# Expert tail: the token table from one-hot products, rows gathered inside the expert stage, one round of experts, answers gathered in two passes

## The reference

```
ln1 = _ln(hidden_states, ln1_weight, ln1_bias)            # attention over the 16 rows that share a column
hidden_after_attn = hidden_states + attn_out @ proj_weight.T
x = _ln(hidden_after_attn, ln2_weight, ln2_bias).reshape(-1, H)     # 4096 tokens, H = 128
probs = softmax(x @ router_weight)                        # 8 experts
top_p, top_i = top_k(probs, 2); top_p = top_p / sum(top_p)
order = argsort(top_i.reshape(-1)); within = position of a pick among its expert's picks
cap = ceil(N * 2 / 8 * 1.25)                              # 1280 slots of each expert, 10240 in all
keep = within < cap; slot = where(keep, expert * cap + within, 8 * cap)
padded_tokens = zeros(8 * cap + 1, H).at[slot].set(x[order // 2])
act = gelu(einsum('ech,ehf->ecf', exp_in, moe_w1))        # F = 512, exact gelu
exp_out = einsum('ecf,efh->ech', act, moe_w2)
moe = zeros(N, H).at[padded_ids].add(exp_out * padded_probs)
out = _layernorm(x_before + hidden_after_attn + moe)
```

## Time and profile before

| | |
|---|---|
| median of 3 runs | 2252.81 us (2251.59 to 2257.84) |
| the profiled execution | 2237.28 us |
| its span, first to last instruction | 2235.5 us |
| granted TensorE clock, mean | 0.88 of full speed |
| busy TensorE, VectorE, ScalarE, GpSimd | 1786.7, 1367.8, 1232.4, 1044.3 us |

### The profile page before, as it was taken

One profiled execution on the slowest core, in us unless ns is written; L12 is line 12 of the kernel. 1 busy time (PEld: TensorE's weight loads), 2 busy tenths in 40 slices (PEclk: granted clock), 3 DMA queues, 4 the chain that ended last, 5 costly groups with the idle time before them and its releaser, 6 DMA issues. The chain is left out here.

```text
span 2235.5 us, 43904 instructions
## 1 busy us (share of the span) xinstructions
PE 1786.7 (80%) x15540; PEld 1384.5 (62%) x15540; DVE 1367.8 (61%) x4497; ACT 1232.4 (55%) x2969; POOL 1044.3 (47%) x1597
## 2 busy tenths in 40 slices
PE   4999999983789999999999999998499980088910
PEld 2666666662567777777777778776356660077900
DVE  4677777752667777777788777875578743000124
ACT  1455555642488777777777777773157750044400
POOL 1456655653155555555555655663214234700066
PEclk8799899986799999999999999998679985589955
DMA  4000000002000000000000000000111000133212
GB/s 52 8 11 13 14 13 13 11 8 80 1 1 2 4 7 6 7 2 6 7 7 7 7 7 4 5 7 6 56 39 40 24 6 24 52 97 95 66 54 66
DMA packets 89818, 52.07 MB, mean 23 GB/s; under 512 B 26944, under 2 KB 83402, under 8 KB 89418
## 3 DMA queue, kind: packets, MB, share of 16 engines
q1 hardware_dynamic: 73682, 38.16, 6.1%
q0 software_dynamic: 4096, 8.40, 1.3%
q10 hardware_dynamic: 11832, 2.80, 0.8%
HBM read 27.31 MB, written 21.50 MB: 22 GB/s over the span
## 5 line engine op out<-in xcount | busy, mean ns | idle before, releaser
L2011 POOL TENSOR_SCALAR probs<-probs,rsums 128x128 f32<-128x128 f32 (+1 forms) x512 | 209.6, 429 | 328.1 <-DVE rsums L1913 328.0
L946 POOL TENSOR_SCALAR at_least<-magnitudes,candidates 128x512 bf16<-128x512 f32 x128 | 198.3, 1569 | 205.9 <-DVE candidates L842 205.9
L1897 DVE CUSTOM_DVE_ANT_0 probs<-dist,pq,nmin 128x128 f32<-128x128 f32 (+1 forms) x512 | 181.0, 408 | 130.6 <-PE pq L1441 130.0
L1670 ACT ACTIVATE probs<-probs,low 128x130 f32<-128x130 f32 (+1 forms) x512 | 227.6, 460 | 4.2 <-DVE low L1897 4.0
L913 DVE TENSOR_REDUCE negmax<-ps_scores 128x4 f32<-128x1024 f32 x128 | 156.5, 1222 | 102.9 <-PE ps_scores L573 101.3
L731 ACT ACTIVATE pT<-ps_scoresT 128x1024 f32<-128x1024 f32 x128 | 131.2, 1025 | 77.6 <-PE ps_scoresT L582 70.4
L2885 DVE COPY m_y<-pm 128x256 f32<-128x256 f32 x40 | 17.0, 425 | 238.2 <-PE pm L2839 238.2
L2969 POOL DMA_INDIRECT f_rows<-expert_answers,idx_get x64 | 61.9, 967 | 197.7 <-PEq L2927 179.2
L1907 DVE COPY pT<-pq 128x384 f32<-128x384 f32 x256 | 129.7, 547 | 2.7 <-PE pq L1456 2.7
L1595 ACT ACTIVATE qn<-pq 128x512 f32<-128x512 f32 x128 | 77.0, 602 | 80.8 <-PE pq L1319 79.2
L1441 PE MATMUL pq<-k1T,q1T 64*128 64x128 f32 (+1 forms) x1024 | 119.7, 352 | 2.1 <-DVE low L1897 2.0
(11 more groups left out here) (511 smaller groups left out, 5564.7 us busy)
## 6 DMA issues: line engine op xcount, KB each, us to landing
expert_rows<-c_zeros SPq DMA_DIRECT2D x8, 640.0 KB, 4.9
m_x<-expert_rows SPq DMA_DIRECT2D x40, 128.0 KB, 2.2
expert_answers<-m_y SPq DMA_DIRECT2D x40, 128.0 KB, 1.9
m_w<-in_L_ffn_moe_w_dram SPq DMA_DIRECT2D x16, 256.0 KB, 4.4
x<-in_x_dram SPq DMA_DIRECT2D x16, 128.0 KB, 2.2
x_mid<-x SPq DMA_DIRECT2D x16, 128.0 KB, 1.9
y<-x_mid SPq DMA_DIRECT2D x16, 128.0 KB, 2.1
x_mid<-y SPq DMA_DIRECT2D x16, 128.0 KB, 1.8
```

Of the source, the lines that this page charges most:

```text
L946: pool.tensor_scalar(at_least[:, a, :], mags[:, 512 * (a // 2):512 * (a // 2) + 512], cf[:, a:a + 1], None, ALU.is_ge).then_inc(mask_ready ...
L1670: ins = act.activation(probs[:, a, keys_nulls(i, w)], probs[:, a, keys_nulls(i, w)], ACT.Exp, bias=low[:, a, i:i + 1], scale=-1.0, accum_o ...
L1897: ins = dve.tensor_tensor_reduce(probs[:, a + t, keys(i, w)], dist[:, (1 - t) * P:N], ps[:, t * P:t * P + w], slopes[h], nmin[u][:, t, h:h ...
L2011: ins = pool.tensor_scalar(probs[:, a + t, keys(i, w)], probs[:, a + t, keys(i, w)], rsums[:, a + t, i:i + 1], 1.0, ALU.mult, ALU.mult)
```

## The change

The tail is rebuilt; `route`, `experts` and `combine` become one function, `moe`, with one block.

In the attention, GpSimd no longer keeps the normalised rows of all groups: they lie in two buffers `hn`, and SyncE stores each group in a DRAM table `token_rows`. For the last group VectorE normalises, after GpSimd's roots. The zero fills are gone. A new step `pick` on VectorE at offset 31 finds the two best experts of each token straight from the logits: at group 6 for columns 0 to 27, at group 7 for the last four.

In `moe` VectorE scans the picks over the columns, TensorE adds the counts of earlier partitions, and VectorE works out for each pick its slot as a tile of 128 slots (80 tiles) and a place in it. For each of the 64 (pick, column) pairs it writes a one-hot row over the 128 places, times the column's number, and a one-hot over the tiles; ScalarE writes the same times the partition's number. TensorE sums 64 products of these, which gives a table of 128 x 160: which token fills each slot. An empty slot gets token 0. GpSimd gathers the rows of each item by two indirect DMAs straight into the item's buffer (8 buffers). All 8 experts' weights are in SBUF, and 40 items run in one round. VectorE makes the gates from the difference of the two logits meanwhile.

Each token's two answers are ordered by slot. The lower ones, which lie in the first seven experts' slots, are gathered when items 0 to 34 are stored, the upper ones when all are. VectorE adds the lower ones to `acc_all`, then goes over the groups: adds the upper ones, takes statistics, makes the roots with shifts and three Newton steps, and ScalarE writes the normalised rows.

```diff
         ] + [(14 + 2 * m, f"heads_T{m}") for m in range(GROUPS)] + [
-            (-7, "lnT"), (-4, "v"), (22, "back"), (23, "project_out"), (29, "hT"), (30, "logits"),
+            (-7, "lnT"), (-4, "v"), (22, "back"), (23, "project_out"), (29, "hT"), (30, "logits"), (31, "pick"),
...
                 moments(u, r[u], 1, half, mv2_ready)
+                if u == U - 1 and half:
+                    dve.wait_ge(*root2_ready.at(1))
+                    for t in range(TG):
+                        dve.tensor_scalar(hn[u][:, t, :], r[u][:, t, :], mv[u][:, 1, t, 0:1],
+                                          rstd[u][:, 1, TG + t:TG + t + 1], ALU.subtract, ALU.mult).then_inc(hn_ready.sem, 1)
+            def pick(u):
...
+                ring.wait_read(dve, "logits", u)
+                src = logits[:, c, :].rearrange("p c e -> p e c")
+                for k in range(2):
+                    top, code, picks = R["top"][:, k, c], R["code"][:, k, c], R["picks"][:, k, :, c]
+                    chain(dve.tensor_reduce(top, src.rearrange("p e c -> p c e"), AX.X, ALU.max))
+                    chain(dve.tensor_tensor(same[:, :, c], src, top.unsqueeze(1).broadcast_to(wide), ALU.is_equal))
+                    chain(dve.tensor_tensor(same[:, :, c], same[:, :, c], R["rev"][:, :, c], ALU.mult))
+                    chain(dve.tensor_reduce(code, same[:, :, c].rearrange("p e c -> p c e"), AX.X, ALU.max))
+                    chain(dve.tensor_tensor(picks, R["rev"][:, :, c], code.unsqueeze(1).broadcast_to(wide), ALU.is_equal))
...
-                    sy.dma_start(spare[:, u * size:(u + 1) * size, :], zeros[:].broadcast_to([P, size, D])).then_inc(zeroed, 16)
...
+                def store_rows(u):
+                    sy.wait_ge(*hn_ready.at(TG * (u + 1)))
+                    sy.dma_start(token_rows[u], hn[u][:]).then_inc(hn_stored[u % 2], 16)
...
-            for c in range(TC):
-                for k in range(2):
-                    pool.indirect_dma_start(out=xs, out_offset=bass.IndirectOffsetOnAxis(ap=idx_put[:, k, c:c + 1], axis=0),
-                                            in_=hn_all[:, c, :], in_offset=None).then_inc(scattered, 16)
-            pool.wait_ge(scattered, 16 * 2 * TC)
...
+        XS, YS, GS = 8, 4, 3
+        ring = Ring(banks[0:7], sem)
...
+            for i in range(2 * TC):
+                if i % (2 * TC // PARTS) == 0:
+                    pe.wait_ge(hot_row_ready, i // (2 * TC // PARTS) + 1)
+                pe.wait_ge(hot_slot_ready, i + 1)
+                mm = pe.matmul(table_ps, hot_slot[:, i, :], hot_tile[:, i].rearrange("p a j -> p (a j)"),
+                               start=(i == 0), stop=(i == 2 * TC - 1))
...
+            dve.tensor_tensor_scan(running[:].rearrange("p e c -> p (e c)"), ..., 0.0, ALU.mult, ALU.add).then_inc(counted, 1)
...
+            for i in range(PARTS):
+                part = slice(size * i, size * (i + 1))
+                dve.tensor_tensor(hot_tile[:, part, 0, :],
+                                  target[:].rearrange("p k c -> p (k c)")[:, part].unsqueeze(2).broadcast_to([P, size, TILES]),
+                                  R["tile_iota"][:].unsqueeze(1).broadcast_to([P, size, TILES]), ALU.is_equal)\
+                    .then_inc(hot_tile_ready, 1)
+                for n in range(size * i, size * (i + 1)):
+                    k, c = divmod(n, TC)
+                    dve.tensor_scalar(hot_slot[:, n, :], R["slot_iota"][:], within[:, k, c:c + 1], float(c + 1),
+                                      ALU.is_equal, ALU.mult).then_inc(hot_slot_ready, 1)
...
+            for n in range(ITEMS):
+                if n >= XS:
+                    ring.wait(pool, "hT", n - XS)
+                for t in range(GT):
+                    j = GT * n + t
+                    pool.indirect_dma_start(out=x[n][:, t, :], out_offset=None, in_=hn_rows,
+                                            in_offset=bass.IndirectOffsetOnAxis(ap=idx_put[:, j:j + 1], axis=0))\
+                        .then_inc(x_loaded[n % XS], 16)
+            pool.wait_ge(idx_get_ready, 1)
+            answers_in(pool, ITEMS - PER)
+            (32 gathers, ys[0:SLOTS - CAP] -> lower[:, c, :])
+            answers_in(pool, ITEMS)
+            for n in range(NG):
+                if n >= GS:
+                    pool.wait_ge(summed, n - GS + 1)
+                (4 gathers, ys -> upper[n][:, t, :])
...
+            for n in range(NG):
+                dve.wait_ge(upper_in[n % GS], 16 * TG * (n // GS + 1))
+                (4 scalar_tensor_tensor, 4 bn_stats, 4 bn_aggr)
+                chain(dve.tensor_scalar(s, mv[:, :, 1], LN_EPS, None, ALU.add))
+                chain(dve.tensor_scalar(q.bitcast(I32), s.bitcast(I32), 1, None, ALU.logical_shift_right))
+                chain(dve.tensor_scalar(q.bitcast(I32), q.bitcast(I32), -1, 0x5f3759df, ALU.mult, ALU.add))
+                for i in range(3):
+                    chain(dve.scalar_tensor_tensor(root[:, 1, :], q, -0.5, q, ALU.mult, ALU.mult))
+                    chain(dve.tensor_tensor(root[:, 2, :], root[:, 1, :], s, ALU.mult))
+                    chain(dve.scalar_tensor_tensor(q, root[:, 2, :], 1.5, q, ALU.add, ALU.mult))
+                dve.scalar_tensor_tensor(turn[n][:, 1, :], mv[:, :, 0], -1.0, q, ALU.mult, ALU.mult).then_inc(turn_ready, 1)
```

More of the change, by code:

```diff
@@ L2132, in column_attention @@
         ln2 = sb("c_ln2", [P, 2])
-        zeros = sb("c_zeros", [P, 1, D])
+        rev_i = sb("c_rev_i", [P, NE, TC], I32)
+        slot_i = sb("c_slot_i", [P, P], I32)
+        tile_i = sb("c_tile_i", [P, TILES], I32)
+        logits = sb("router_logits", [P, TC, NE])
+        same = sb("c_same", [P, NE, TC])
+        rest = sb("c_rest", [P, NE, TC])
         ident_r = sb("c_ident_r", [P, P], F32R)
@@ new lines, in moe @@
+        kept = sb("m_kept", [P, 2, TC])
+        slot = sb("m_slot", [P, 2, TC])
+        ends = sb("m_ends", [P, 2, TC])
+        idx_get = sb("m_idx_get", [P, 2, TC], I32)
+        gap = sb("m_gap", [P, TC])
+        gates = sb("m_gates", [P, 3, TC])
+        swap = sb("m_swap", [P, 2, TC])
+        gate_w = sb("m_gate_w", [P, 2, TC])
+        hot_slot = sb("m_hot_slot", [P, 2 * TC, P], BF16)
+        hot_tile = sb("m_hot_tile", [P, 2 * TC, 2, TILES], BF16)
+        found = sb("m_found", [P, 2, TILES])
@@ L2878, in _ @@
-        @block.vector
-        def _(dve):
-            with dve.Fori(0, NE // U) as it:
-                for n in range(ITEMS):
-                    if n >= YS:
-                        dve.wait_ge(stored[n % YS], 16 * (n // YS))
-                    ps = ring.wait(dve, "down", n)
-                    dve.tensor_copy(y[n][:].rearrange("p t d -> p (t d)"), ps[:, 0:GT * D]).then_inc(y_ready.sem, 1)
-                    dve.wait_ge(*y_ready.at(n + 1))
-                    dve.sem_inc(ring.read("down", n), 1)
-                meet.join(dve, "vector")
@@ L2963, in _ @@
+            rows(0)
+            for n in range(ITEMS):
+                if n + 1 < ITEMS:
+                    rows(n + 1)
+                if n >= 2:
+                    ring.wait(act, "down", n - 2)
+                for half in range(2):
+                    ps = ring.wait(act, "up", n, half)
+                    act.activation(hid[n][:, 2 * half:2 * half + 2, :].rearrange("p c n -> p (c n)"), ps[:],
+                                   ACT.Gelu).then_inc(ring.read("up", n, half), 1)
             for n in range(NG):
+                act.wait_ge(turn_ready, n + 1)
@@ new lines, in _ @@
+            for k in range(2):
+                chain.add(dve.tensor_tensor(spread[:, k], picks[:, k].rearrange("p e c -> p c e"),
+                                            running[:].rearrange("p e c -> p c e"), ALU.mult))
+            dve.wait_ge(chain.sem, chain.n)
+            chain(dve.tensor_reduce(rank[:], spread[:], AX.X, ALU.add))
+            chain(dve.tensor_scalar(rank_i[:], rank[:], 1.0, None, ALU.subtract))
+            chain(dve.tensor_scalar(tile_i[:], rank_i[:], 7, None, ALU.logical_shift_right))
@@ new lines, in _ @@
+            chain(dve.tensor_tensor(gates[:, 0, :], gates[:, 0, :], kept[:, 1, :], ALU.mult))
+            chain(dve.tensor_tensor(gates[:, 2, :], gates[:, 0, :], gates[:, 1, :], ALU.subtract))
+            chain(dve.tensor_tensor(swap[:, 1, :], gates[:, 2, :], swap[:, 0, :], ALU.mult))
+            chain.add(dve.tensor_tensor(gate_w[:, 0, :], gates[:, 1, :], swap[:, 1, :], ALU.add))
+            chain(dve.tensor_tensor(gate_w[:, 1, :], gates[:, 0, :], swap[:, 1, :], ALU.subtract))
+            for n in range(ITEMS):
+                if n >= YS:
+                    dve.wait_ge(stored[n % YS], 16 * (n // YS))
+                ps = ring.wait(dve, "down", n)
+                dve.tensor_copy(y[n][:].rearrange("p t d -> p (t d)"), ps[:, 0:GT * D]).then_inc(y_ready.sem, 1)
+                dve.wait_ge(*y_ready.at(n + 1))
+                dve.sem_inc(ring.read("down", n), 1)
```

495 lines of the change are left out of this document (223 added, 272 removed).

## The result

The changed kernel takes 2175.2 us (median of four runs, 2161.4 to 2192.1) against 2253.2 for the kernel before on the same chip: a ratio of 0.970, 95% interval 0.964 to 0.976. I had forecast 2143, range 2128 to 2168. The direction was right; 29% of the gain (32 us of 110) did not arrive. The profiled run took 2161.35 us, with a span of 2159.6.

A forecast was written before the change was run, and what follows sets the result against it. The tail was taken as a chain of routing, scatters, experts and gathers, engines not sharing work. Costs and gains summed to 109.7 us less than the profiled 2237.3, 2127.6; plus 15.5 to the median, 2143 us, range 2128 to 2168.

The forecast's parts named there:

- Before the routing: Attention's end: finding the two best experts there starts the next stage at 1858.2 instead of 1854.0, +4.2 us.
- To the first expert rows: Slot table and first gathers: 24.9 us to the first gather, first transposes at 1887.0 instead of 1964.4.
- p: Price of one bf16 one-hot operation of 128 elements on VectorE: taken as 0.17 us, bounds 0.10 and 0.28.
- the bound: One-hot block: VectorE's 17.0 us was to decide; TensorE's 64 products beside it were put at 15 us in all.
- The experts, "155.1": Forty items in one round at 3.73 us each: 155.1 us against 165.8, 10.7 gained.
- rivals 4 and 5: Gathers pace everything: at 2 us each a median of 2201, chance 0.04; at 2.7 us 2302, slower, chance 0.02.
- my 5.7: Last stage: VectorE's time per group with waits, 5.7 us against 5.0 for four gathers; eight groups 45.6 us.
- Against it: Skill's claim that VectorE's two-port operations lock GpSimd's descriptor writing, 620 ns becoming 3100; set aside, as no row agreed.
- VectorE without waits between upper groups: Sign expected in the last stage of the profile after, where VectorE was to become the bound.
- the lower gathers: Sign expected at the experts' end: they begin some 14 us before the last answer copy.

The follow-up runs named there:

- x14: The changed kernel with a one-column GpSimd operation after each of its 144 indirect gathers: 2135.2 us, ratio 0.951.
- x6: The changed kernel with the 32 lower additions split, four ahead of each group's four upper ones, instead of one block: 2175.5 us, one run.
- x15: The changed kernel with expert rows loaded in plain order by direct 64 KB DMAs on GpSimd's queue, not gathered: 2131.3 us, one run.
- x1: The changed kernel with expert rows loaded in plain order by SyncE's direct 64 KB DMAs, not gathered: 2141.4 us, ratio 0.952.

## Why the prediction was wrong

**Before the routing: right.** The second pick began at 1851.71, 2.8 us ahead of the forecast; its twelve operations (eleven counted) took 2.75 us against 2.5. The 2.8 us lie within the spread of this program's first part, so they confirm and refute nothing. **To the first expert rows: right**, 24.5 us from the stage's start against 24.9: scan 0.69 (0.5), one-hot part 2.04 us (2.13), p between two starts 0.17 (0.17), TensorE's eight products 1.25 us in all and far from the bound. The estimate of 0.09 for p that the Trainium skill gives ("VectorE: DVE Perf Modes", section on the TRN2 errata) was rightly not followed.

**The experts, "155.1": right for the work, wrong in the trace.** The items ran at 3.73 and a granted clock of 1.00. The step that failed is the silent one beneath the sum: "Two gathers an item are 2.5 us, under TensorE's 3.73, and eight buffers lie between" costs the gathers as GpSimd's time and holds that their only effect is when rows arrive. They have another: in a row 1.25 us apart they slow TensorE, VectorE and ScalarE to one instruction in 0.70 us or stop them (TensorE for 25 us before 2078.27), and for this the sum had nothing. x14 against the changed kernel measures it: 34 us. By what means the row does this stays open. The trace of before could hardly show it: its scatters stood alone, its experts had no indirect DMA beside them, and its last stage waited for the gathers anyway. My rivals 4 and 5 doubted the price of a gather, which was 0.95 and 0.30 as read; none doubted its neighbours.

Counted from the first gather, the miss of 36.8 us (279.5 against 242.7) splits so. The first gap delays the first lower gather by 15.4 us (160.1 against 144.7). The second delays the last copy by a further 31, but most of it lies under the lower gathers; the upper ones begin 24.0 us late, so it costs 8.6. The lock of the first upper gather costs 5.9, less 0.1 by rounding: the first group starts 29.8 late. In the last stage groups are 0.52 us cheaper than my 5.7, eight times, -4.2; starving costs 12.6; from there to the end 1.4 less. 29.8 - 4.2 + 12.6 - 1.4 = 36.8. In the gaps TensorE, nearly or wholly idle, also fell to 1.2 GHz (granted clock 0.50 from 1902.3 to 1916.0 and from 2055.9 on), and its first eight wide products after the first gap took 3.78 us where they take 1.89 at 2.4 GHz. That is counted in the terms above.

x14 is the test of the rest of the sum. With every gap gone the tail was 245.9 us against the 242.7 forecast, and its first upper gather comes 4.7 us late for the 32 rests ahead of it. What I had worked out was right to about 3 us; what I had left out was 34 us or more.

**"Against it": wrong for the kernel as it ran.** I set aside the Trainium skill, "SBUF — State Buffer", section "Who interferes with whom", because no row of before agreed. The page has an exclusive lock on a shared pair of ports, held for a whole instruction, and counts operations with two inputs in SBUF among those that contend with GpSimd's reads. A gather reads its indices from SBUF. x6 agrees with such a lock: it is worth 5.9 us where 32 additions stand together. Eight together do not hold a gather, before or in x6 (1.09 us at most). This gather of before began with a block of eight that ran from 2155.26 to 2157.57:

```profile
2155.27 1.09 POOL L2969 DMA_INDIRECT f_rows<-expert_answers,idx_get  x1 [0.19 <-issue]
```

Why 32 hold it and eight do not, no run shows. On the forecast's own timeline, with the last copy 26 us before the last lower gather, the block would not have formed, and x14's first upper gather took 0.96 us. So the lock was not the step that failed: it came with the second gap.

**"VectorE without waits between upper groups"** held for all but the second and third; **the lower gathers**, counted on to begin some 14 us before the last copy, did start before it, and in the undisturbed x14 by 13.4 us.

## What to carry to other kernels

Where indirect DMAs are moved beside other engines' work, their price is not only GpSimd's time: look whether "remote" or "issue" gaps in steps of 0.7 us appear on several engines at once while they run. If they do, try one tiny dependent operation after every indirect DMA before smarter scheduling: here it took 0.14 us each and gave back 34. A stretch without instruction packets proves nothing by itself: compare it with the same piece of program in a run without the gap. And let VectorE's two-input operations not stand together in a long block where GpSimd is about to issue (32 cost 5.9 us, eight 0.14).

## What was not expected of the hardware

- A row of indirect gathers 1.25 us apart slowed or stopped TensorE, VectorE and ScalarE, in the second gap from 2047.4 to 2085.4 us, at a DMA share of 0.24; 1.39 us apart, with a small operation between, it did not. I first took this for instruction packets kept out. The Trainium skill, "DMA: Bandwidth & Descriptors", section "Queues, rings and completion order", has each DMA engine take turns between its queues, one packet at a time. By that rule a refill would wait for a few packets only, and no trace here shows one that waited longer. What does hold the engines up no run here shows. That 0.14 us more suffice, that a rest each fourth gather or a pause of 3.9 us does not, and that x15 escaped, I can report and not explain.
- An engine so disturbed goes on at 0.70 us per instruction, waits included, or stands, VectorE for up to 33 us (x1, before its last but one copy).
- Gathers in which a fifth of the rows are one and the same row take 2.4 times as long in the DMA engines (38.9% against 16.0% for 704 packets), and no gap moved when that was mended.
